# Slot attention: the next stage's weights sent in four pieces within the second pass, the context rows of group 2 sent before the first wait, and whole key transfers for all groups but the third

## The chip, the cores and the metric

The kernel runs on one core of one Trainium2 chip. The metric is the device time of one execution in microseconds. A core has TensorE (PE: matmuls into PSUM), the vector engine (DVE), ScalarE (ACT), GpSimd (POOL) and a sync engine (SP) that here only issues transfers. Transfers are issued on a queue of SP's or of ACT's own and are carried out by the same 16 DMA engines. The engines wait for each other by semaphores.

## What is computed

A network of four layers and twelve stages over 128 rows of 256 numbers, in which several stages attend to one context of 12544 keys. The change lies in the first stage, slot attention: three passes over all keys, each followed by a gated recurrent update of the 128 slots.

```
for _ in range(NUM_ITERS):                       # 3
    sn = rmsnorm(slots, slot_norm_w)
    q = jnp.einsum('bkd,ed->bke', sn, Wq)
    scores = jnp.einsum('bkd,bmd->bkm', q, k_proj) * scale
    attn = jax.nn.softmax(scores, axis=-2)
    attn = attn / (jnp.sum(attn, axis=-1, keepdims=True) + EPS)
    updates = jnp.einsum('bkm,bmd->bkd', attn, v_proj)
    slots = gru_cell(updates, slots, gru_wi, gru_wh, gru_bi, gru_bh)
```

`k_proj` and `v_proj` are projections of the context after a root-mean-square norm of each row. The softmax runs over the slots, so each key is a row of its own.

## The kernel before

**Tiles.** The 12544 keys are 14 groups of 896 (7 tiles of 128). A pass goes over the 14 groups; n counts them through the three passes, 0 to 41. Two layouts of the context are used. `ctxT` (numbers by keys, 896 KB a group) feeds the scores and is loaded anew in every pass into two buffers that alternate. `ctx_rows` (keys by numbers, 896 KB a group) feeds the weighted sum; it is loaded once, in pass 1, and kept.

**A group's way.** TensorE scores the group, first a half of 4 tiles and then one of 3 (`BANK_TILES`, L155 by way of `product`), and signals `scored` after each. The vector engine takes maxima (L531) and scales them by the roots `rinv` (L535). ScalarE takes the exponentials (L493), half by half, and signals `exp`. The vector engine normalises the probabilities (L545). TensorE multiplies them with the rows (`attend`, L388) and the vector engine adds the result to `pooled` (L549). TensorE's order is written out: score(n), then attend(n - 2), so at the start of a pass three groups are scored before the first attend.

**Only in pass 1** the roots are made: after the first half of exponentials of group n, ScalarE squares four tiles of the rows of group n + 1 (L486), the vector engine the other three (L558), and GpSimd raises the mean squares to -0.5 (L361, L363). The maxima of group n + 1 wait for its roots. The squares are written behind the home of the weights "patt", where "quant_up" comes later.

**SP's program** (L339 to L351) is one list of transfers in the order of n. For each n it waits until the half of group n - 2 that the buffer held has been scored, and sends the half (L346); then it sends the rows that `ROWS_AT` names for this n (L337). The 2560 KB of "gates" (weights of the update) follow at n = 10. Groups 0 and 1 need no wait. Each half has its own semaphore, `ctxT_in` with buffer and half, and TensorE waits for it before it scores the half.

**Weights of later stages** lie in one region with fixed homes (`HOMES`). `Weights.fetch` (L115) sends one whole and `Weights.wait` waits for its semaphore. "patt" (4100 KB, 8200 numbers on each of 128 partitions) is for the second stage and "quant_up" (768 KB) for the third; both are sent by ScalarE at the start of pass 2, before its first exponential. The vector engine rounds "quant_up" in small steps (`up.some`) in the spare time of passes 2 and 3.

**Before the first score** TensorE waits for the weights "slots", multiplies two of them (`fold_qk`, twice), transposes the slots and forms the query. `idle_products` (L171) multiplies the identity with constants into a bank that nobody reads.

## Time and profile before

| | us |
|---|---|
| median of three runs | 1555.98 |
| lowest and highest of them | 1551.15, 1556.0 |
| the profiled execution, time | 1554.31 |
| its span in the profile | 1552.4 |
| TensorE busy in it | 1441.7 (93%) |
| the vector engine, ScalarE, GpSimd busy | 929.9, 765.2, 80.9 |
| data moved | 182.30 MB, mean 117 GB/s |

The span is cut by time from its own start. Slot attention takes it from 4 to 326 us: first score at 13.53, second pass from 121.02, third from 230.05. A timeline row tells start, duration, engine, line, the operation with what it writes and reads, the number of instructions merged, and in brackets the engine's idle time just before and what ended it. The granted clock of TensorE is a share of 2.4 GHz, so 0.50 is 1.2 GHz. A line that a helper holds (L155, L346) has many users; the names of the tiles tell them apart. An fp32 matmul leaves two records.

### The profile page before, as it was taken

Reading aid. Unit: us, or ns where it says so; the run is one execution under the profiler, and the core shown is the slowest. Engines: PE = TensorE matmul, PEld = TensorE weight load, DVE = VectorE, ACT = ScalarE, POOL = GpSimd, SP = SyncE. Lnnn points to the kernel's source line nnn. Section 1 sums busy time; section 2 is a strip of 40 time slices with the busy share of each in tenths; the row PEclk is TensorE's granted clock in tenths of the full one; section 3 lists DMA queues with packets and bytes.
Section 4 is the critical chain, followed back from the end, with each engine's and each line's share of the span. In section 5 each row is a group of like instructions: output and inputs, shape, how many; then the busy total and the mean of one; then the engine's idle time right before and its main releaser. Section 6 shows DMA issues by size and latency. Waiting matters only on the chain. (4 is left out here: it accounts for less than half of the span.)

```text
span 1552.4 us, 29696 instructions
## 1 busy us (share of the span) xinstructions
PE 1441.7 (93%) x11376; PEld 1097.2 (71%) x11376; DVE 929.9 (60%) x2890; ACT 765.2 (49%) x1793; POOL 80.9 (5%) x78
## 2 busy tenths in 40 slices
PE   7997999988899789999999999999998798889987
PEld 6987989965677554677777677777776695656765
DVE  4754556656666432577777777777777375444434
ACT  5854536523122131467766676667667771323222
POOL 2310000000000000200000000000000000000000
PEclk9998999997999999999999999999999998989999
DMA  9946425311247289311111111110000301407860
GB/s 295 363 148 238 152 73 172 114 41 70 113 174 279 95 317 349 138 37 37 37 37 37 37 37 37 37 37 29 10 1 2 126 2 44 189 0 265 269 252 4
DMA packets 82812, 182.30 MB, mean 117 GB/s; under 512 B 5872, under 2 KB 58608, under 8 KB 81264
## 3 DMA queue, kind: packets, MB, share of 16 engines
q1 hardware_dynamic: 81952, 171.98, 31.5%
q10 hardware_dynamic: 720, 8.42, 1.3%
q8 instruction: 92, 1.51, 0.4%
q14 instruction: 48, 0.39, 0.1%
HBM read 179.86 MB, written 0.52 MB: 116 GB/s over the span
## 5 line engine op out<-in xcount | busy, mean ns | idle before, releaser
L2052 ACT ACTIVATE cross_s<-cross_s,cross_shift 128x896 f32<-128x896 f32 x224 | 215.1, 1031 | 35.1 <-DVE cross_shift L2136 35.1
L2046 ACT COPY cross_eT<-cross_ring 128x512 f32<-128x512 f32 x280 | 153.2, 591 | 143.2 <-PE cross_ring L1974 143.2
L1974 PEld LDWEIGHTS cross_ring<-consts,cross_s 128*128 128x128 f32 x1568 | 169.7, 142 | 58.8 <-issue 43.6
L1974 PE MATMUL cross_ring<-consts,cross_s 128*128 128x128 f32 x1568 | 198.3, 279 | 8.7 <-ACT cross_s L2052 8.7
L2127 DVE CUSTOM_DVE_ANT_0 cross_s<-cross_scores,cross_mask,cross_top 128x448 f32<-128x448 f32 x224 | 141.3, 680 | 83.2 <-PE cross_scores L1966 83.1
L493 ACT ACTIVATE slots_probs<-slots_scores,slots_bias,ctx_rinv 128x128 f32<-128x128 f32 x294 | 130.3, 458 | 105.1 <-DVE slots_bias L535 105.0
L155 PE MATMUL slots_scores<-slots_qkT,slots_ctxT 128*128 128x128 f32 x1176 | 142.0, 280 | 8.8 <-DMA slots_ctxT<-in_ctxT 8.2
L2127 DVE CUSTOM_DVE_ANT_0 cross_s<-cross_scores,cross_mask,cross_half_max 128x448 f32<-128x448 f32 x224 | 141.3, 680 | 14.7 <-PE cross_scores L1966 14.7
L155 PEld LDWEIGHTS slots_scores<-slots_qkT,slots_ctxT 128*128 128x128 f32 x1176 | 140.7, 197 | 12.3 <-DMA slots_ctxT<-in_ctxT 9.4
L388 PE MATMUL slots_attended<-ctx_rows,slots_probs 128*128 128x257 f32 x588 | 134.2, 380 | 2.4 <-DVE slots_probs L545 1.5
L388 PEld LDWEIGHTS slots_attended<-ctx_rows,slots_probs 128*128 128x128 f32 x588 | 108.6, 190 | 17.7 <-DVE slots_probs L545 1.9
L1966 PE MATMUL cross_scores<-cross_keysT,cross_qz 32*128 32x448 f32 x896 | 118.4, 586 | 1.3 <-DVE cross_qz L2097 1.3
L1988 PEld LDWEIGHTS cross_attended<-cross_eT,cross_values 128*32 128x32 f32 x3136 | 82.3, 110 | 38.0 <-issue 35.8
L531 DVE TENSOR_REDUCE slots_top<-slots_scores 128x4 f32<-128x512 f32 x84 | 52.4, 623 | 85.4 <-PE slots_scores L155 85.3
L1988 PE MATMUL cross_attended<-cross_eT,cross_values 128*32 128x128 f32 x3136 | 97.2, 274 | 2.3 <-ACT cross_eT L2046 1.7
L2109 DVE COPY cross_eT<-cross_ring 128x512 f32<-128x512 f32 x112 | 77.5, 692 | 34.4 <-PE cross_ring L1974 34.4
L155 PE MATMUL cross_ring<-weights_region,cross_ctxT 128*128 128x256 f32 x364 | 84.6, 384 | 0.0
L155 PE MATMUL cross_ring<-cross_ctxT,weights_region 128*128 128x448 f32 x208 | 83.5, 544 | 0.0
L155 PEld LDWEIGHTS cross_ring<-weights_region,cross_ctxT 128*128 128x128 f32 x364 | 67.0, 190 | 9.1
L1922 POOL TENSOR_SCALAR cross_mask<-cross_mask_int 128x896 f32<-128x896 int32 x14 | 44.9, 3205 | 458.0 <-DVE cross_top L2127 452.0
L1966 PEld LDWEIGHTS cross_scores<-cross_keysT,cross_qz 32*128 32x128 f32 x896 | 36.4, 182 | 38.3 <-issue 29.8
L493 ACT ACTIVATION_READ_ACCUMULATOR slots_probs<-slots_scores,slots_bias,ctx_rinv 128x1 f32 x294 | 60.0, 204 | 0.0
(805 smaller groups left out, 2111.2 us busy)
## 6 DMA issues: line engine op xcount, KB each, us to landing
ctx_rows<-in_ctx_rows SPq DMA_DIRECT2D x28, 896.0 KB, 7.7
ctx_rows<-in_moe_w SPq DMA_DIRECT2D x24, 1024.0 KB, 9.6
slots_ctxT<-in_ctxT SPq DMA_DIRECT2D x42, 512.0 KB, 4.0
slots_ctxT<-in_ctxT SPq DMA_DIRECT2D x42, 384.0 KB, 4.6
cross_ctxT<-in_ctxT SPq DMA_DIRECT2D x13, 896.0 KB, 4.7
padded_ctxT<-in_ctxT SPq DMA_DIRECT2D x12, 896.0 KB, 4.6
plain_ctxT<-in_ctxT SPq DMA_DIRECT2D x12, 896.0 KB, 4.7
local_layers<-in_w_local SPq DMA_DIRECT2D x2, 4552.0 KB, 13.8
```

Source lines behind the costliest of these rows:

```text
L155: last = pe.matmul(out, lhs, rhs, start=i == 0, stop=i == len(pairs) - 1)
L388: last = pe.matmul(at[b], probs[:, n % HELD, t], K.ctx[:, g * TILE + t, :], start=t == 0, stop=t == TILE - 1)
L493: last = act.activation(probs[:, a, t], sc[b][:, t], ACT.Exp, bias=bias[:, a, t:t + 1], scale=K.rinv[:, g * TILE + t:g * TILE + t + 1], ac ...
L531: dve.tensor_reduce(top[:, a, own], sc[b][:, own], X_AXIS, ALU.max).then_inc(st("top"), 1)
L1922: pool.tensor_scalar(mask[:, g % 2], mask_int[:, g % 2], 0.0, MASKED, ALU.is_equal, ALU.mult).then_inc(st("mask"), 1)
L1966: pe.matmul(scores(j), qz[rows, s // 2, s % 2], keysT[rows, g % 2, s // 2, half_keys(half)], start=True, stop=True).then_inc(st("scored"), 1)
L1974: last = pe.transpose(bank(("turn", u, t))[:, j * P:(j + 1) * P], s_buf[:, u % 2, j, t * P:(t + 1) * P], K.ident)
L1988: last = pe.matmul(attended[COLS * j:COLS * (j + 1), s * P:(s + 1) * P], values[:, g % 2, t, set_head(s, j)], eT[:, u % 2, t, j * P:(j + 1 ...
L2046: act.copy(eT[:, u % 2, t], bank(item)).then_inc(st("emptied_act"), 1)
L2052: act.activation(rows, rows, ACT.Exp, bias=shift[:, u % 2, j:j + 1], scale=SCALE).then_inc(st("exp"), 1)
L2109: dve.tensor_copy(eT[:, u % 2, t], bank(item)).then_inc(st("emptied_dve"), 1)
L2127: dve.tensor_tensor_reduce(s_buf[:, u % 2, j, half_keys(half)], scores(j), mask[:, g % 2, half_keys(half)], 1.0, so_far, ALU.add, ALU.max, ...
```

## The change

It has five edits, all in slot attention and the weights' fetch.

1. "patt" is sent as four pieces of 2050 columns (1025 KB each), by ScalarE after the exponentials of groups 3, 5, 7 and 9 of pass 2 (`PATT_AT`, `fetch_piece`); its semaphore counts four. "quant_up" is sent after the exponentials of group 0 of pass 2, with the same waits ahead of it.
2. `ROWS_AT`: the rows of group 2 go out at n = 1, right behind those of group 1. Rows 3 to 6 go out one a step at n = 2 to 5, rows 7 and 8 at n = 6, the others as before.
3. The keys of a group go out as one transfer when both halves of group n - 2 have been scored. Only the third group of each pass (`SPLIT_GROUP`) keeps its two halves and their two waits.
4. Two idle products stand ahead of TensorE's first wait.
5. The vector engine's steps on "quant_up" begin at group 4 of pass 2 instead of group 3, and one more is taken in pass 3.

```diff
--- before.py
+++ after.py
@@ -114,8 +114,13 @@
     def fetch(self, eng, name):
         eng.dma_start(self.buf(name), self.T[f"w_{name}"]).then_inc(self.arrived[name], 16)
 
+    def fetch_piece(self, eng, name, i, pieces):
+        spec, at = HOMES[name]
+        n = width(spec) // pieces
+        eng.dma_start(self.region[:, at + i * n:at + (i + 1) * n], self.T[f"w_{name}"][:, i * n:(i + 1) * n]).then_inc(self.arrived[name], 16)
+
     def wait(self, eng, name):
-        eng.wait_ge(self.arrived[name], 16)
+        eng.wait_ge(self.arrived[name], 16 * PIECES.get(name, 1))
 
 
 def linked(eng, sem):
@@ -240,8 +245,10 @@
 HELD = SLOT_LAG + 1
 ACT_ROWS = 4
 ROWS_SENT = 4
-ROWS_AT = {1: [1], 2: [2], 3: [3, 4], 4: [5, 6], **{n: [n + 2] for n in range(5, GROUPS - 2)}}
+ROWS_AT = {1: [1, 2], **{n: [n + 1] for n in range(2, 6)}, 6: [7, 8], **{n: [n + 2] for n in range(7, GROUPS - 2)}}
+PATT_AT = (3, 5, 7, 9)
 BANK_TILES = (range(0, 4), range(4, TILE))
+SPLIT_GROUP = 2
 
 
 class Quantise:
@@ -324,6 +331,12 @@
         def tiles(g):
             return slice(g * TILE, (g + 1) * TILE)
 
+        def sent_parts(n):
+            return BANK_TILES if n % GROUPS == SPLIT_GROUP else (range(TILE),)
+
+        def transfers(n, s):
+            return sum(len(sent_parts(m)) > s for m in range(n % 2, n + 1, 2))
+
         def rows_in(g):
             return st(f"rows_in{g % (ROWS_SENT + 1)}")
 
@@ -339,9 +352,9 @@
                 load_rows(0)
                 for n in range(SLOT_ITERS * GROUPS):
                     g, b = n % GROUPS, n % 2
-                    for s, part in enumerate(BANK_TILES):
+                    for s, part in enumerate(sent_parts(n)):
                         if n >= 2:
-                            sp.wait_ge(st("scored"), 2 * (n - 2) + s + 1)
+                            sp.wait_ge(st("scored"), 2 * (n - 2) + (s + 1 if g == SPLIT_GROUP else 2))
                         keys = slice(part[0] * P, part[-1] * P + P)
                         sp.dma_start(ctxT[:, b, :, keys], T["ctxT"][g:g + 1, :, :, keys].rearrange("o p c m -> p (o c) m")).then_inc(st(f"ctxT_in{b}{s}"), 16)
                     if n in ROWS_AT:
@@ -369,7 +382,8 @@
                 def score(n):
                     b = n % 2
                     for s, part in enumerate(BANK_TILES):
-                        pe.wait_ge(st(f"ctxT_in{b}{s}"), (n // 2) * 16 + 16)
+                        if s < len(sent_parts(n)):
+                            pe.wait_ge(st(f"ctxT_in{b}{s}"), 16 * transfers(n, s))
                         if n >= 2:
                             pe.wait_ge(st("exp"), 2 * (n - 2) + s + 1)
                         for t in part:
@@ -407,6 +421,7 @@
                 def update_slots(k):
                     pe.matmul(update, slotsT[:, k], wh[:, k, D:2 * D], start=False, stop=False)
 
+                idle_products(pe, K, scores[:, 1536:2048], 2)
                 K.weights.wait(pe, "slots")
                 fold_qk(0)
                 for it in range(SLOT_ITERS):
@@ -501,15 +516,16 @@
                     act.activation(small[:, 2:3], small[:, 1:2], ACT.Sqrt).then_inc(st("rms"), 1)
                     if it == 0:
                         squares(0)
-                    if it == 1:
-                        K.weights.fetch(act, "patt")
-                        act.wait_ge(st("squares_act"), ACT_ROWS * GROUPS)
-                        act.wait_ge(st("squares_dve"), (TILE - ACT_ROWS) * GROUPS)
-                        K.weights.fetch(act, "quant_up")
                     for g in range(GROUPS):
                         if g >= HELD:
                             act.wait_ge(st("attended"), it * GROUPS + g - HELD + 1)
                         exponentials(it * GROUPS + g)
+                        if it == 1 and g == 0:
+                            act.wait_ge(st("squares_act"), ACT_ROWS * GROUPS)
+                            act.wait_ge(st("squares_dve"), (TILE - ACT_ROWS) * GROUPS)
+                            K.weights.fetch(act, "quant_up")
+                        if it == 1 and g in PATT_AT:
+                            K.weights.fetch_piece(act, "patt", PATT_AT.index(g), PIECES["patt"])
                     act.wait_ge(st("reset_mm"), it + 1)
                     act.activation(gate[:, 0:D], reset, ACT.Sigmoid).then_inc(st("reset"), 1)
                     act.wait_ge(st("cand_in"), it + 1)
@@ -606,10 +622,10 @@
                             last.then_inc(st("gate_rows"), 1)
                         if g >= 1 + SLOT_LAG:
                             add(n - 1 - SLOT_LAG)
-                        if it == 1 and 3 <= g < GROUPS:
+                        if it == 1 and 4 <= g < GROUPS:
                             up.some(dve, 1)
                         if it == 2 and g < GROUPS:
-                            up.some(dve, 2 if g < 4 else 1)
+                            up.some(dve, 2 if g < 5 else 1)
 
                     link(dve.reciprocal(small[:, 5:6], pooled[:, D:D + 1]))
                     dve.tensor_scalar(diag[:, :], K.ident, small[:, 5:6], None, ALU.mult).then_inc(st("pooled"), 1)
@@ -3092,6 +3108,7 @@
     "delta": (DELTA_SPEC, max(DIAGONALS * P, width(FOLD_SPEC) + width(MOE_SPEC) + width(CROSS_SPEC))),
     "mqa": (MQA_SPEC, 0), "hashed": (HASH_SPEC, width(MQA_SPEC)),
 }
+PIECES = {"patt": 4}
 EARLY = {"padded": 2, "cross": 1, "plain": 2}
 EARLY_AT = {"padded": HOMES["padded"][1] + width(PADDED_SPEC), "cross": HOMES["cross"][1] + width(CROSS_SPEC) + SLOT_W1 + SLOT_W2,
             "plain": HOMES["hashed"][1]}
```

SP's queue at the start of the stage. Names: `ctx_rows` are the kept rows, `slots_ctxT` the key buffers; 128x2x512 is the first half of a group, 128x2x384 the second, 128x1792 a whole group. Before:

```order
L337 DMA ctx_rows<-in_ctx_rows 128x7x256
L346 DMA slots_ctxT<-in_ctxT 128x2x512
L346 DMA slots_ctxT<-in_ctxT 128x2x384
L346 DMA slots_ctxT<-in_ctxT 128x2x512
L346 DMA slots_ctxT<-in_ctxT 128x2x384
L337 DMA ctx_rows<-in_ctx_rows 128x7x256
L346 DMA slots_ctxT<-in_ctxT 128x2x512 [waits slots_scored]
L346 DMA slots_ctxT<-in_ctxT 128x2x384 [waits slots_scored]
L337 DMA ctx_rows<-in_ctx_rows 128x7x256
```

And now:

```order
L350 DMA ctx_rows<-in_ctx_rows 128x7x256
L359 DMA slots_ctxT<-in_ctxT 128x1792 x2
L350 DMA ctx_rows<-in_ctx_rows 128x7x256 x2
L359 DMA slots_ctxT<-in_ctxT 128x2x512 [waits slots_scored]
L359 DMA slots_ctxT<-in_ctxT 128x2x384 [waits slots_scored]
L350 DMA ctx_rows<-in_ctx_rows 128x7x256
L359 DMA slots_ctxT<-in_ctxT 128x1792 [waits slots_scored]
L350 DMA ctx_rows<-in_ctx_rows 128x7x256
```

The two key transfers of groups 0 and 1 are whole, rows of group 2 stand ahead of the first wait, and group 3's keys (the last but one row) wait for both halves of group 1.

ScalarE at the start of pass 2, from the root that the query needs (`slots_small`) on. The waits of a row stand in brackets. Before:

```order
L501 ACTIVATE slots_small<-slots_small 128x1 [waits slots_ms]
L115 DMA weights_region<-in_w_patt 128x8200
L115 DMA weights_region<-in_w_quant_up 128x1536 [waits slots_squares_dve,slots_squares_act]
L493 ACT_TABLE_LOAD
L493 ACTIVATE slots_probs,slots_total<-slots_scores,slots_bias,ctx_rinv 128x128 [waits slots_bias]
L493 ACTIVATE slots_probs,slots_total<-slots_scores,slots_bias,ctx_rinv 128x128 x3
L493 ACTIVATE slots_probs,slots_total<-slots_scores,slots_bias,ctx_rinv 128x128 [waits slots_bias]
L493 ACTIVATE slots_probs,slots_total<-slots_scores,slots_bias,ctx_rinv 128x128 x2
```

And now:

```order
L516 ACTIVATE slots_small<-slots_small 128x1 [waits slots_ms]
L508 ACT_TABLE_LOAD
L508 ACTIVATE slots_probs,slots_total<-slots_scores,slots_bias,ctx_rinv 128x128 [waits slots_bias]
L508 ACTIVATE slots_probs,slots_total<-slots_scores,slots_bias,ctx_rinv 128x128 x3
L508 ACTIVATE slots_probs,slots_total<-slots_scores,slots_bias,ctx_rinv 128x128 [waits slots_bias]
L508 ACTIVATE slots_probs,slots_total<-slots_scores,slots_bias,ctx_rinv 128x128 x2
L115 DMA weights_region<-in_w_quant_up 128x1536 [waits slots_squares_dve,slots_squares_act]
```

Both weight transfers stood ahead of the table load and the first exponential; now "quant_up" follows the seven exponentials of the first group. The first piece of "patt" stands behind those of the fourth, in front of the fifth's:

```order
L508 ACTIVATE slots_probs,slots_total<-slots_scores,slots_bias,ctx_rinv 128x128 [waits slots_bias]
L508 ACTIVATE slots_probs,slots_total<-slots_scores,slots_bias,ctx_rinv 128x128 x2
L120 DMA weights_region<-in_w_patt 128x2050
L508 ACTIVATE slots_probs,slots_total<-slots_scores,slots_bias,ctx_rinv 128x128 [waits slots_bias,slots_attended]
L508 ACTIVATE slots_probs,slots_total<-slots_scores,slots_bias,ctx_rinv 128x128 x3
```

The other three pieces stand in the same way behind groups 5, 7 and 9.

## Rows read from the trace of the kernel before

**Rows 1.** Stretches: length, busy us (records) of PE, PEld, DVE, ACT, POOL, clock, DMA share, GB/s.

```profile
13.53:106.73 93.20, 89.90 (x588) 82.63 (x589) 61.07 (x199) 66.69 (x301) 26.67 (x42) 0.98 0.87 295
121.02:217.48 96.46, 89.08 (x589) 83.43 (x589) 49.33 (x122) 45.97 (x197) 0.00 (x0) 0.95 0.53 176
230.05:316.42 86.37, 86.37 (x590) 80.89 (x590) 52.43 (x128) 45.89 (x197) 0.00 (x0) 1.00 0.42 129
```

**Rows 2.** Timeline of TensorE at the starts of passes 2 and 3.

```profile
134.81 5.85 PE L155 MATMUL slots_scores<-slots_qkT,slots_ctxT 128*128 128x128 f32 x28 [7.38 <-DMA slots_ctxT<-in_ctxT]
140.50 3.21 PE L388 MATMUL slots_attended<-ctx_rows,slots_probs 128*128 128x257 f32 x14
...
239.43 3.21 PE L388 MATMUL slots_attended<-ctx_rows,slots_probs 128*128 128x257 f32 x14
```

**Rows 3.** Stretches of 1 us, TensorE alone: busy (records), clock, DMA share, GB/s.

```profile
130.00:131.00 1.00, 0.00 (x0) 0.50 0.96 395
...
140.00:141.00 1.00, 1.00 (x9) 1.00 0.75 172
```

**Rows 4.** Transfers, 117 to 134.8: queue, packets, MB, share; issues, KB, us to landing.

```profile
q10 hardware_dynamic: 288, 4.98, 69.9%
q1 hardware_dynamic: 789, 1.40, 20.8%
...
weights_region<-in_w_patt ACTq DMA_DIRECT2D x1, 4100.0 KB, 14.0
...
slots_ctxT<-in_ctxT SPq DMA_DIRECT2D x2, 384.0 KB, 11.0
```

**Rows 5.** Transfers issued at 233 to 235, at 19 to 20, and in a later stage.

```profile
slots_ctxT<-in_ctxT SPq DMA_DIRECT2D x1, 384.0 KB, 4.6
...
ctx_rows<-in_ctx_rows SPq DMA_DIRECT2D x1, 896.0 KB, 7.8
...
padded_ctxT<-in_ctxT SPq DMA_DIRECT2D x12, 896.0 KB, 4.6
```

**Rows 6.** Timeline of TensorE, start of the stage and pass 1.

```profile
5.93 2.08 PE L155 MATMUL slots_mm<-weights_region 128*128 128x256 f32 x4 [5.93 <-DMA weights_region<-in_w_slots]
...
10.72 1.13 PE L155 MATMUL slots_attended<-slots_qk_weight,slots_slotsT 128*128 128x256 f32 x4 [0.58 <-DVE slots_qk_weight L563]
...
25.93 3.31 PE L388 MATMUL slots_attended<-ctx_rows,slots_probs 128*128 128x257 f32 x14 [0.83 <-DVE slots_probs L545]
...
33.00 3.31 PE L388 MATMUL slots_attended<-ctx_rows,slots_probs 128*128 128x257 f32 x14 [0.64 <-DVE slots_probs L545]
...
40.12 3.28 PE L388 MATMUL slots_attended<-ctx_rows,slots_probs 128*128 128x257 f32 x14 [0.69 <-DVE slots_pooled L549]
...
46.97 3.21 PE L388 MATMUL slots_attended<-ctx_rows,slots_probs 128*128 128x257 f32 x14
...
81.52 3.39 PE L155 MATMUL slots_scores<-slots_qkT,slots_ctxT 128*128 128x128 f32 x28 [0.50 <-DMA slots_ctxT<-in_ctxT]
```

**Rows 7.** Stretches, TensorE alone, columns as in rows 3.

```profile
128.00:134.80 6.80, 0.00 (x0) 0.63 1.01 399
42.00:66.00 24.00, 23.66 (x164) 1.00 1.06 357
16.00:18.00 2.00, 2.00 (x15) 0.72 0.10 30
```

**Rows 8.** Timeline of SP's queue, the issues of two transfers.

```profile
19.16 0.61 SPq L337 DMA_DIRECT2D ctx_rows<-in_ctx_rows  x1
...
66.90 1.19 SPq L115 DMA_DIRECT2D weights_region<-in_w_gates  x1
```

**Rows 9.** Timeline of ScalarE and GpSimd in pass 1.

```profile
26.99 0.42 ACT L486 ACTIVATE weights_region<-ctx_rows 128x256 f32<-128x256 f32 x1 [1.31 <-DMA ctx_rows<-in_ctx_rows]
...
29.07 1.48 POOL L363 TENSOR_TENSOR ctx_rinv<-slots_ms,slots_power 128x7 f32<-128x7 f32 x1
...
34.72 1.48 POOL L363 TENSOR_TENSOR ctx_rinv<-slots_ms,slots_power 128x7 f32<-128x7 f32 x1
```

## Prediction

> **What bounds the kernel now.** The edits touch the first stage, slot attention, which runs three passes over 14 groups of keys. I read the table of stretches first [rows 1]: the part of passes 1, 2 and 3 from the first score to the last attend. All three do the same TensorE work (588 to 590 matmul records), and only pass 3 is TensorE without a gap: 86.37 us busy of 86.37, clock 1.00, 6.17 us a group. So pass 3 is the floor and the others show their losses: pass 2 takes 96.46, which is 10.09 too long, and pass 1 takes 93.20, which is 6.83 too long. TensorE bounds the stage; where it stands still, the time adds to the end. The later stages keep their instructions and start when this one ends.
>
> Pass 2's loss is in one place. In TensorE's timeline [rows 2] it waits 7.38 us for keys at the third group, and then needs 5.7 us for that group's 28 records (134.81 to 140.50), where pass 3 needs 9.38 for three groups, 3.1 each. The clock's rows [rows 3] say why: granted 0.50 (1.2 GHz) after TensorE had stood still, 1.00 (2.4 GHz) again only at 140. From 121.02 to the first attend at 140.50 are 19.48 us; in pass 3 they are 9.38, from 230.05 to 239.43 [rows 1, 2]. The difference, 10.10, is the whole loss of pass 2. The cause is in the transfers [rows 4]: the smaller half of a group's keys took 11.0 us to land where it takes 4.6 in pass 3 [rows 5], because the next stage's weights, 4100 KB that landed after 14.0 and another 768 KB, were sent on ScalarE's queue just before the first score.
>
> Pass 1's loss is spread [rows 6]. Attends start at 25.93, 33.00, 40.12 and 46.97, so 12.40 us from the first score (9.38 in pass 3), then 7.07, 7.12 and 6.85 where 6.17 is the floor: losses of 3.02, 0.90, 0.95 and 0.68. A wait of 0.50 at 81.52, behind the gates' weights, is the next. These are 6.05 of the 6.83; the rest lies around the gates and at the end of the pass.
>
> **Part 1, weights in pieces.** The big transfer leaves the start of pass 2 and goes out as four of 1025 KB, after the exponentials of groups 3, 5, 7 and 9; the 768 KB one goes after those of group 0. Without them the third group's halves land as in pass 3, and TensorE reaches the first attend 10.1 us earlier: the half clock goes with the wait. What is late next is the fourth group's keys: one transfer, issued when the second group is scored and needed 6.17 later. A whole 896 KB transfer lands in 4.6 in a later stage [rows 5]; the 768 KB now beside it add 0.786 MB at 399 GB/s, the rate of the crowded stretch [rows 7], so 2.0 us. 4.6 + 2.0 is 6.6 against 6.17: a wait between 0 and 0.5, I take 0.3.
> The pieces: a steady group's keys are issued when the group two before is scored (3.1 us of its 6.17) and needed 12.34 - 3.1 = 9.2 us later. 4.6 plus the whole of a piece, 1.05 MB at 399 GB/s = 2.6, is 7.2. That leaves 2.0 us, so the pieces cost nothing; the cover is TensorE's own two attends and one score, and if it were gone a piece would cost its 2.6. Their issue lies on a ScalarE that is busy 46 of 96 us [rows 1]. Nothing reads these weights before the next stage. The vector engine's rounding steps move by one group in a pass where it is busy 49 of 96: nothing.
> Part 1: -10.1 + 0.3 = **-9.8 us**.
> The queues' rows [rows 4] also show what a turn carries: 288 packets took 4.98 MB on ScalarE's queue (17 KB each), 789 took 1.40 MB on sync's (1.8 KB each). The Trainium skill, "DMA: Bandwidth & Descriptors", section "Queues, rings and completion order", says that a DMA engine takes turns between the queues packet by packet. By that rule the keys starved for their small packets, and whole transfers beside quarter pieces, with packets of like size, would share evenly: the sum stays, and rival (c) loses weight.
>
> **Part 2, rows sent ahead.** Rows of group 2 now go out with those of group 1, before sync first waits for a score. Today they are issued at 19.2 [rows 8] and land 7.8 later, at 27.0 [rows 5], and ScalarE, which squares them, waits for them: its squares start at 26.99 after 1.31 idle [rows 9]. The DMA engines stood nearly empty from 16 to 18 us, 30 GB/s for the 357 of full stretches [rows 7]; the rows (0.92 MB at 357, 2.6 us) fill that hole and land near 19.5. Then GpSimd's root for group 2, which ends at 30.55 [rows 9], ends 1.3 earlier, and attend 1 is released by TensorE itself: 33.00 becomes 32.1. The root of group 3 follows one loop later (36.20 - 30.55 = 5.65), so at 34.9 for 36.2, and attend 2 with it: 40.12 becomes 38.8. For attend 3 the keys come in time, since the rows of groups 6 and 7 no longer stand ahead of them: 6.17, so 44.9 for 46.97, **-2.1 us**. The third group's own halves now queue behind the moved rows: 18.7 + 1.5 + about 1 is 21.2, when TensorE gets to them at 21.7. No cost.
>
> **Part 3, one transfer per group but the third.** The first half of a group's keys goes out 1.3 us later than now, the second at the same time. In steady parts the 9.2 us cover it, in all three passes. It bites where the slack is short, behind the gates' weights. There TensorE wanted the first half at 81.0 and got it at 81.5 [rows 6]; the second (0.39 MB at 357) came 1.1 later. A whole transfer ends with the second: a wait of 1.6 for 0.5, unless the queue is less full than now. It is: the filled hole moves its work 2 us or more forward while TensorE moves 2.1. From its own issue, 1.2 us before the gates' at 66.90 [rows 8], the chain is 65.7 + 4.6 (keys) + 2.6 (rows) + 6.6 (gates, 2.62 MB at 399) + 2.3 (keys) = 81.8. Between -0.1 and +1.1; I take **+0.2**.
>
> **Part 4, two idle products.** They run from 4.1 to 6.1 by the duration of four such records at 5.93, 2.08 us [rows 6], where TensorE waits for weights until 5.93 anyway: **+0.1**. Whether they bring the full clock earlier is the first rival.
>
> Sum: -9.8 - 2.1 + 0.2 + 0.1 = -11.6 us. The profiled execution took 1554.3 (span 1552.4 and 1.9 around it), so it becomes **1542.7**. It stood 1.7 under the median of the three runs and 3.2 over their lowest; I keep 1542.7.
>
> **Rivals.** (a) The idle products warm the clock. For it: four records of 256 columns take 2.08 us from 5.93 and 1.13 from 10.72 [rows 6], after TensorE has been busy for a while; starting 1.8 us earlier could bring the rise before the second fold, which lies on the path, and start the scores at 12.1 for 13.53. Against it: the clock falls again, to a mean of 0.72 in 16 to 18 [rows 7], and the third group's keys do not land before 21, so the first attend comes at 24.1 at best, for 25.93. TensorE then runs ahead of the transfers and waits longer at the gates, 1.1. Net -1.8 - 0.3 (no wait at attend 2) + 1.1 = -1.0: 1541.7, or 1540.6 without that longer wait.
> The Trainium skill, "TensorE: Matmul & The Clock Gate", section "What's actually happening", says that the throttled clock is the default and activity releases it; by that rule this rival happens.
> (b) The transfers collide more than I say, without a fall of the clock: 0.5 at the fourth group for 0.3, 1.1 at the gates for 0.2, 1 us in pass 1 because the rows of groups 5 to 7 go out later than now, and half of part 2 missing (1.0). Together +3.1: 1545.8.
> (c) Slower: each piece holds up the keys beside it as the whole did. If they landed after 11.0 as in [rows 4], TensorE would wait 11.0 - 9.2 = 1.8 and lose 2.6 more at half clock (5.7 - 3.1), 4.4 four times, 17.6: 1560.3. It beats the gain from 2.9 us a piece on. Against it: a piece is a fifth of what did that.
> (d) The moved rows and idle products do nothing at all: 1544.8.
>
> **Numbers.** The forecast 0.42, (a) 0.27, (b) with (d) 0.28, (c) 0.03. The range runs from 1538.5 ((a) at its best, less the 1.7 between runs) to 1548 ((b), plus as much). A measurement tells 0.3%, 4.7 us, from no change; all but (c) lie beyond it: faster 0.95, same 0.03, slower 0.02.
>
> **What would show it.** Part 1: pass 2's stretch at 86.4 to 87.2 with clock 1.00, no wait for keys above 0.5, four pieces landing in 5 to 8 us. Part 2: rows of group 2 landing near 19.5, no ScalarE idle before their squares, attends 6.17 apart but for the second. Part 3: one wait of 0.4 to 1.6 behind the gates. Part 4: first score at 13.5 (12.1 by rival a). Pass 1's stretch at 91 to 92. It is wrong if pass 2 stays over 90, or if a stage behind this one changes its length by more than 1 us.

## The result, and the profile after

The changed kernel took **1546.19 us** (median of 20 runs, 1540.65 to 1551.29) beside 1555.57 for the kernel before (20 runs, 1548.13 to 1559.38): a ratio of 0.9944, 95% interval 0.9932 to 0.9956, so 9.4 us faster. The profiled execution took 1549.58 us with a span of 1547.7, which is 3.4 over its own median. The span before was 1552.4, so the two profiled executions differ by 4.7 us only; where these lie is told behind the experiments.

The three passes, from the first score to the last attend, in the table of stretches that [rows 1] has for the kernel before (columns as there):

```profile
15.76:106.87 91.11, 89.61 (x588) 82.76 (x589) 60.92 (x199) 66.58 (x301) 26.71 (x42) 1.00 0.83 294
121.16:211.01 89.85, 86.89 (x589) 81.03 (x589) 49.11 (x121) 45.98 (x197) 0.00 (x0) 1.00 0.56 200
223.58:310.45 86.87, 86.62 (x589) 80.96 (x589) 52.61 (x129) 45.88 (x197) 0.00 (x0) 1.00 0.38 128
```

Pass 1 went from 93.20 to 91.11, pass 2 from 96.46 to 89.85, pass 3 from 86.37 to 86.87. Pass 2 is still 3 us or more above its floor of 86.4 to 86.9, and TensorE's timeline shows the loss in two waits on the third group's keys, where [rows 2] had one of 7.38:

```profile
121.16 6.41 PE L160 MATMUL slots_scores<-slots_qkT,slots_ctxT 128*128 128x128 f32 x56
128.58 2.05 PE L160 MATMUL slots_scores<-slots_qkT,slots_ctxT 128*128 128x128 f32 x16 [1.01 <-DMA slots_ctxT<-in_ctxT]
132.58 1.60 PE L160 MATMUL slots_scores<-slots_qkT,slots_ctxT 128*128 128x128 f32 x12 [1.95 <-DMA slots_ctxT<-in_ctxT]
134.03 3.21 PE L402 MATMUL slots_attended<-ctx_rows,slots_probs 128*128 128x257 f32 x14
137.07 3.29 PE L160 MATMUL slots_scores<-slots_qkT,slots_ctxT 128*128 128x128 f32 x28
```

The first 14 records of the attend after the waits take 3.21 us, and the granted clock reads 1.00 in every stretch of 1 us from 128 to 135, so the clock did not fall here. The fourth group's keys, for which I had forecast the wait, made none (137.07 has no bracket). They landed 7.1 us after their issue, later than the 6.6 I had for them, but TensorE itself came 3 us late by then. The transfers issued from 117 to 134.8, to be held against [rows 4], and then those issued while a piece was sent, 141 to 147 (queue: packets, MB, share; issue: KB, us to landing):

```profile
q1 hardware_dynamic: 688, 1.84, 31.4%
q10 hardware_dynamic: 144, 0.79, 12.3%
...
slots_ctxT<-in_ctxT SPq DMA_DIRECT2D x2, 896.0 KB, 5.8
weights_region<-in_w_quant_up ACTq DMA_DIRECT2D x1, 768.0 KB, 6.8
slots_ctxT<-in_ctxT SPq DMA_DIRECT2D x1, 512.0 KB, 5.4
slots_ctxT<-in_ctxT SPq DMA_DIRECT2D x1, 384.0 KB, 8.1
...
q1 hardware_dynamic: 144, 0.92, 44.8%
q10 hardware_dynamic: 135, 1.03, 42.9%
...
weights_region<-in_w_patt ACTq DMA_DIRECT2D x1, 1025.0 KB, 6.8
slots_ctxT<-in_ctxT SPq DMA_DIRECT2D x1, 896.0 KB, 5.2
```

The second half of the third group (384 KB) landed 8.1 us after its issue, for 11.0 before and 4.6 undisturbed [rows 4, 5]. ScalarE's timeline tells what met it:

```profile
124.06 0.46 ACT L508 ACTIVATE slots_probs<-slots_scores,slots_bias,ctx_rinv 128x128 f32<-128x128 f32 x1 [4.68 <-DVE slots_bias L551]
...
125.29 0.20 ACT L508 ACTIVATION_READ_ACCUMULATOR slots_probs<-slots_scores,slots_bias,ctx_rinv 128x1 f32 x1
125.34 0.38 ACTq L115 DMA_DIRECT2D weights_region<-in_w_quant_up  x1
...
127.03 0.22 ACT L508 ACTIVATION_READ_ACCUMULATOR slots_probs<-slots_scores,slots_bias,ctx_rinv 128x1 f32 x1
```

The code puts this transfer after the seven exponentials of group 0. They end at 127.25, but the issue stands at 125.34, while the third of the seven ends: ScalarE's queue hands the transfer out while activations ahead of it in the program still have to run. The other two profiles of this kernel show the same, and so does the first piece, issued at 141.21 during the exponentials of group 3. The issue at 125.34 is about 1 us behind that of the half that landed late (between 124.4 and 124.6), and 1.9 earlier than the code reads.

Pass 1's steps add up to what was forecast: attends at 28.29, 34.95, 41.11 and 47.29, so steps of 6.66, 6.16 and 6.18, 19.0 in sum, where [rows 6] gave 7.07, 7.12 and 6.85, 21.0 in sum. The wait behind the gates is 0.31 for 0.50:

```profile
28.29 3.31 PE L402 MATMUL slots_attended<-ctx_rows,slots_probs 128*128 128x257 f32 x14 [0.36 <-DVE slots_probs L561]
...
34.95 3.21 PE L402 MATMUL slots_attended<-ctx_rows,slots_probs 128*128 128x257 f32 x14
...
41.11 3.22 PE L402 MATMUL slots_attended<-ctx_rows,slots_probs 128*128 128x257 f32 x14
...
47.29 3.21 PE L402 MATMUL slots_attended<-ctx_rows,slots_probs 128*128 128x257 f32 x14
...
81.66 3.39 PE L160 MATMUL slots_scores<-slots_qkT,slots_ctxT 128*128 128x128 f32 x28 [0.31 <-DMA slots_ctxT<-in_ctxT]
```

The mechanism that was forecast for these steps is there too. ScalarE has no idle time before it squares the rows of group 2, and GpSimd's root for them, which follows, ends at 31.49:

```profile
30.01 1.48 POOL L376 TENSOR_TENSOR ctx_rinv<-slots_ms,slots_power 128x7 f32<-128x7 f32 x1
```

That is 15.73 us after the first score, for 17.02 before (30.55 less 13.53): 1.3 earlier, as forecast.

The pass begins 2.2 us later than before, though (15.76 for 13.53). In this execution the weights "slots" landed about 1.1 us later (first product of the fold at 6.98 for 5.93), and the query's products, with the transposes behind them, ran at half rate (another 1.2):

```profile
6.98 2.08 PE L160 MATMUL slots_mm<-weights_region 128*128 128x256 f32 x4 [0.70 <-DMA weights_region<-in_w_slots]
...
9.27 1.91 PE L160 MATMUL slots_mm<-weights_region 128*128 128x256 f32 x4
11.76 2.08 PE L160 MATMUL slots_attended<-slots_qk_weight,slots_slotsT 128*128 128x256 f32 x4 [0.58 <-DVE slots_qk_weight L579]
```

In [rows 6] the row that answers to the last took 1.13. The slow query products stand in no other profiled execution of any kernel here; weights that came late do in two more (6.83 and 6.56). Neither is laid to the change, and together they are 2.2 of the 3.4 by which this execution stands over the median. The granted clock reads 1.00 over these rows, so the half rate is told from their durations alone.

### The profile page after: what moved, and what is told of

Read it like the earlier page. It is cut to its first block and busy times, and to the rows that moved or that the text cites. A ratio compares the mean times of both kernels' runs of the same rounds, so it can differ in the third digit from the quotient of the medians.

```text
span 1547.7 us, 29631 instructions
## 1 busy us (share of the span) xinstructions
PE 1442.9 (93%) x11380; PEld 1096.2 (71%) x11380; DVE 929.7 (60%) x2890; ACT 765.1 (49%) x1793; POOL 80.9 (5%) x78
```

## The experiments

All were timed beside the kernel before on the same chip (before: 1554.69, 1555.24 and 1555.40 in the three sets), and each left one profiled execution. The changed kernel itself was in the first and the third set; runs of the second set are held against all 32 runs of it. Theory Q is the one from the trace above: what is left of pass 2's loss is the 768 KB transfer, issued into the third group's halves.

**The changed kernel again**, in the first and the third set.

> The changed kernel once more, as the base of this call and as a second sample of its start. Theory L (luck at the start): the late first score of the first execution (15.8 us for 13.5 in the kernel before) is no part of the change; here it may come anywhere between 12.5 and 16, and the time is 9 us under the kernel before. Theory P (the products): the two idle products hold the fold back, so the first score is again past 15 us. Both: TensorE again waits near 1.0 and 1.9 us for the third group's halves in pass 2, whose stretch takes 89 to 90 us.

> The changed kernel beside the two that follow, on one chip. Both theories: 1545.5 to 1546.5 as the earlier runs of it, pass 2 between 88.5 and 90 us with key waits of 1.8 to 3.0 us on the third group and none after.

Measured: 1545.54 (1540.68 to 1551.84; 0.9940, 0.9921 to 0.9959) and 1546.37 (1543.15 to 1548.86; 0.9940, 0.9923 to 0.9957). Waits in pass 2: 0.99 + 0.86 and 0.76 + 1.78, both times on the third group; the pass took 88.74 and 89.43. First scores at 13.28 and 13.56: the late start of the first profile was luck.

**The 768 KB two groups later**, twice.

```diff
-                        if it == 1 and g == 0:
+                        if it == 1 and g == 2:
                             act.wait_ge(st("squares_act"), ACT_ROWS * GROUPS)
```

> The changed kernel with the 768 KB weights sent after the exponentials of group 2 of pass 2 instead of group 0. Theory Q (those 768 KB hold the third group's two halves up, since ScalarE's queue issues them 1.8 us before the last exponential of the group ends): both waits go, pass 2's stretch falls from 89.9 to 86.4 to 86.9, and the time falls by 3.0 us against the changed kernel (ratio about 0.992 to the kernel before). Rival W (the whole transfers of groups 3 and on, which stand in sync's queue, hold the halves up): the waits stay at 2 us or more and the time does not move.

> The kernel of e1_up_late once more (in_w_quant_up sent two groups later), beside the changed kernel on this chip. Theory Q (the wait is the 768 KB meeting the third group's halves): 2 to 4 us below the changed kernel, key waits in pass 2 below 1.0 us in sum, pass 2 at 86.4 to 87.5 us. Rival (the 3 us of the first pair was luck of the run): within 1 us of the changed kernel's time.

Measured: 1542.88 (1537.18 to 1547.39; 0.9922, 0.9904 to 0.9941) and 1544.28 (1539.57 to 1548.23; 0.9926, 0.9908 to 0.9943), 2.7 and 2.1 under the changed kernel on the same chip. The means of the 12 runs of each differ by 2.6 +- 2.7 us; against all 32 runs of the changed kernel the 12 are 2.8 +- 2.3 lower. The profile shows where: the wait before the second half is gone in both, and pass 2 takes 87.44 and 87.67. TensorE's timeline of the second run, then the transfers it issued from 118 to 136:

```profile
118.85 6.41 PE L160 MATMUL slots_scores<-slots_qkT,slots_ctxT 128*128 128x128 f32 x56
126.31 3.39 PE L160 MATMUL slots_scores<-slots_qkT,slots_ctxT 128*128 128x128 f32 x28 [1.04 <-DMA slots_ctxT<-in_ctxT]
129.54 3.21 PE L402 MATMUL slots_attended<-ctx_rows,slots_probs 128*128 128x257 f32 x14
```

```profile
weights_region<-in_w_quant_up ACTq DMA_DIRECT2D x1, 768.0 KB, 5.5
slots_ctxT<-in_ctxT SPq DMA_DIRECT2D x1, 512.0 KB, 5.4
slots_ctxT<-in_ctxT SPq DMA_DIRECT2D x1, 384.0 KB, 5.1
```

The second half lands after 5.1 for 8.1. Theory Q holds for the second wait. The first half still lands after 5.2 to 5.4 with no weights under way (issue of the 768 KB at 130.60), and costs 0.8 to 1.0.

**The same transfer, only held back until the exponentials have ended.**

```diff
                         if it == 1 and g == 0:
+                            act.wait_ge(st("exp"), 2 * GROUPS + 2)
                             act.wait_ge(st("squares_act"), ACT_ROWS * GROUPS)
```

> The changed kernel with one more wait ahead of the 768 KB transfer: ScalarE first waits until its own last exponential of group 0 has ended. The prediction had put the issue there (127.1 on the time scale of the kernel before), while the trace shows it 1.8 us earlier, in the middle of the seven exponentials. Theory Q: issued 1.8 us later, it no longer meets the third group's second half: that one lands 4.6 to 5.5 after its issue for 6.9 and 8.1, and the wait falls on the fourth group's keys, 0 to 0.5 us as predicted; pass 2's stretch 87 to 88, 1 to 2 us under the changed kernel. Rival T (the 1.8 us are too little, what counts is the turn-taking of two queues with any transfer of the third or fourth group): total waits in pass 2's first four groups stay at 1.8 us or more, only later in place.

Measured: 1547.81 (1541.41 to 1550.23; 0.9941, 0.9921 to 0.9961). This is the place at which I had supposed the issue. TensorE's timeline, then the issue in ScalarE's:

```profile
127.53 3.39 PE L160 MATMUL slots_scores<-slots_qkT,slots_ctxT 128*128 128x128 f32 x28 [0.92 <-DMA slots_ctxT<-in_ctxT]
130.75 3.21 PE L402 MATMUL slots_attended<-ctx_rows,slots_probs 128*128 128x257 f32 x14
134.38 3.39 PE L160 MATMUL slots_scores<-slots_qkT,slots_ctxT 128*128 128x128 f32 x28 [0.42 <-DMA slots_ctxT<-in_ctxT]
```

```profile
126.07 0.22 ACT L508 ACTIVATION_READ_ACCUMULATOR slots_probs<-slots_scores,slots_bias,ctx_rinv 128x1 f32 x1
126.31 0.38 ACTq L115 DMA_DIRECT2D weights_region<-in_w_quant_up  x1
126.75 0.46 ACT L508 ACTIVATE slots_probs<-slots_scores,slots_bias,ctx_rinv 128x128 f32<-128x128 f32 x1 [0.46 <-ACT slots_probs L508]
```

With the issue behind the exponentials the wait on the second half is gone and one of 0.42 stands at the fourth group, where the prediction had 0.3. So the mechanism and the size were right for the place I thought of, and the place was wrong. In the time nothing can be told from the changed kernel (the means agree within 0.2, +- 3); pass 2 took 88.24 here, and 88.74 to 89.85 in the changed kernel.

**The pieces alone** on the kernel before: the edits of part 1 (four pieces, the 768 KB after group 0's exponentials, the rounding steps), with the old rows, halves everywhere and no idle products.

```diff
-                    if it == 1:
-                        K.weights.fetch(act, "patt")
...
                         exponentials(it * GROUPS + g)
+                        if it == 1 and g == 0:
...
+                            K.weights.fetch(act, "quant_up")
+                        if it == 1 and g in PATT_AT:
+                            K.weights.fetch_piece(act, "patt", PATT_AT.index(g), PIECES["patt"])
```

> The kernel before with the weights' edit alone: four pieces of the 4100 KB and the 768 KB after group 0, all key transfers in halves, rows in the old order, no idle products. By my steps it carries nearly the whole gain: pass 2's stretch 89 to 91 for 96.5, -6 to -7.5 us, ratio 0.9955. Rival W: with halves everywhere the pieces' large packets starve the keys' small ones, so TensorE waits up to 2 us behind each of the four pieces and pass 2 stays at 92 to 98.

Measured: 1548.69 (1547.13 to 1549.24; 0.9958, 0.9945 to 0.9971), 6.0 us under before. Pass 2 takes 90.73. TensorE's timeline, then the stretches of 1 us (busy, clock, DMA share, GB/s):

```profile
130.81 1.73 PE L160 MATMUL slots_scores<-slots_qkT,slots_ctxT 128*128 128x128 f32 x12 [2.42 <-DMA slots_ctxT<-in_ctxT]
132.33 4.81 PE L394 MATMUL slots_attended<-ctx_rows,slots_probs 128*128 128x257 f32 x14
```

```profile
131.00:132.00 1.00, 1.00 (x10) 1.00 1.01 380
132.00:133.00 1.00, 1.00 (x6) 0.58 1.01 384
133.00:134.00 1.00, 1.00 (x3) 0.50 0.34 112
```

86.4 (the floor) + 2.42 (the wait) + 1.6 (14 products in 4.81 for 3.21) is 90.4 of the 90.73. The half clock came after this one wait; after the changed kernel's 1.01 and 1.95, with 16 records between, it did not. At the pieces themselves TensorE never waits, though the 384 KB halves of that stretch need 7.0 us in the median. No run sends the 4100 KB whole at a later place, so how much of the gain is the place and how much the cutting is not shown.

**The rows alone, and the rows put back.** First the new table on the kernel before, then the old table on the changed kernel.

```diff
-ROWS_AT = {1: [1], 2: [2], 3: [3, 4], 4: [5, 6], **{n: [n + 2] for n in range(5, GROUPS - 2)}}
+ROWS_AT = {1: [1, 2], **{n: [n + 1] for n in range(2, 6)}, 6: [7, 8], **{n: [n + 2] for n in range(7, GROUPS - 2)}}
```

> The kernel before with the new order of the rows alone. By my steps attends 0 to 3 of pass 1 are 6.2, 6.6 and 6.2 apart (7.07, 7.12, 6.85 before), pass 1's stretch is 91 for 93.2, and the time is 2.1 us lower, ratio 0.9987, at the edge of what five rounds tell. Rival: the moved rows hold up the third group's halves in sync's queue, TensorE waits for them and the first attend comes as much later as the next ones gain: stretch 93, ratio 1.000.

> The changed kernel with the old table of context rows (one row group late in the places 1 to 6). Theory R (the rows sent ahead are worth what the first pass lost before): the late rows come back, pass 1 is 92 to 93.5 us instead of 90.4 to 91.1, and the time is 1.5 to 2.5 us above the changed kernel's. Rival (what the rows give, the clock or the next wait takes back, as where they were put alone): pass 1 is longer but the time within 1 us of the changed kernel's.

Measured: alone 1554.0 (12 runs, 1549.51 to 1559.63; 0.9995, 0.9984 to 1.0006); put back 1549.95 (1547.06 to 1551.77; 0.9962, 0.9947 to 0.9977), 3.6 over the changed kernel on the same chip (against all 32 runs of it the means differ by 3.3 +- 2.0). With the old table the attends of pass 1 drift apart again. TensorE's timeline of the kernel with the rows put back:

```profile
31.57 3.21 PE L402 MATMUL slots_attended<-ctx_rows,slots_probs 128*128 128x257 f32 x14
35.81 3.39 PE L160 MATMUL slots_scores<-slots_qkT,slots_ctxT 128*128 128x128 f32 x28 [1.03 <-DMA slots_ctxT<-in_ctxT]
39.04 3.21 PE L402 MATMUL slots_attended<-ctx_rows,slots_probs 128*128 128x257 f32 x14
43.25 3.39 PE L160 MATMUL slots_scores<-slots_qkT,slots_ctxT 128*128 128x128 f32 x28 [1.01 <-DMA slots_ctxT<-in_ctxT]
46.48 3.21 PE L402 MATMUL slots_attended<-ctx_rows,slots_probs 128*128 128x257 f32 x14
```

Steps of 7.47 and 7.44 for 6.16 and 6.18; the pieces alone, with the same table, have 7.62 and 7.46. So the rows are worth 2.6 us in those two steps, and it is the keys, queued behind rows that were not yet needed, that end them.

Alone on the kernel before, the moved rows did what was expected in the trace: steps of 6.27, 6.50 and 6.24, 19.0 in sum for 21.0. Pass 1 was even shorter than that (13.52 to 102.90, so 89.38 for 93.20), but 1.3 of these 3.8 us lie ahead of the first attend, where the first scores happened to run at full clock. That part varies by itself: from the first score to the first attend the thirteen profiled executions took 11.1 to 13.6 us. From the first attend to the end of the pass they took 80.80 before, 81.55 and 81.11 in the two other kernels with the old table, and 78.1 to 79.3 with the new table, with one exception (below, without idle products). So the rows are worth about 2.5 us in the trace, with the other edits or without. The median alone moved by 0.7 only, the means by 0.8 +- 1.8, which 2.1 does not contradict, nor is it far enough from 3.3 +- 2.0 to be called another value. In that one profile pass 3 also began with products at half rate (L405, the reset gate's product, took 1.90 for 1.03, the first 84 records of scores 10.38 for 9.5) and was 0.8 longer; one profile can't tell whether this is the rule.

The moved rows have a price, too, that the prediction put at nothing. With the old table TensorE never waited for the third group's keys in pass 1. With the new one it waited 0.41 and 0.80 in two of the changed kernel's three profiles, 0.85 with the rows alone, and 1.58 to 2.21 in four of the other variants, whose first scores had run at full clock.

**Halves everywhere** in the changed kernel (part 3 undone).

```diff
-            return BANK_TILES if n % GROUPS == SPLIT_GROUP else (range(TILE),)
+            return BANK_TILES
-                            sp.wait_ge(st("scored"), 2 * (n - 2) + (s + 1 if g == SPLIT_GROUP else 2))
+                            sp.wait_ge(st("scored"), 2 * (n - 2) + s + 1)
```

> The changed kernel with every group's keys in two halves again (84 transfers), all else kept. My step for this part said +0.2 us for whole transfers, so -0.2 here, nothing that can be told: ratio 0.994. In the trace: behind the gates' weights the wait is 0 to 0.5, while the pieces' packets of 8 KB meet keys' packets of 2 KB, so that the halves beside a piece land in 6 to 8 us for the 4.6 of a whole transfer, still inside their 9.2. Rival W2 (whole transfers carry a gain of their own, by fewer and larger packets in the full stretches of pass 1): pass 1's stretch is 1 us or more longer than the 90.4 to 91.1 of the changed kernel.

Measured: 1547.45 (1544.52 to 1550.13; 0.9947, 0.9932 to 0.9962). The means differ from the changed kernel's by 1.1 +- 1.9: nothing that can be told. But the transfers differ. In the window from 110 to 165 of this kernel, and then of the changed one:

```profile
slots_ctxT<-in_ctxT SPq DMA_DIRECT2D x8, 512.0 KB, 4.8
slots_ctxT<-in_ctxT SPq DMA_DIRECT2D x7, 384.0 KB, 7.5
weights_region<-in_w_patt ACTq DMA_DIRECT2D x2, 1025.0 KB, 7.1
```

```profile
slots_ctxT<-in_ctxT SPq DMA_DIRECT2D x6, 896.0 KB, 4.6
weights_region<-in_w_patt ACTq DMA_DIRECT2D x2, 1025.0 KB, 6.5
```

Taken one by one over the whole pass, the four halves of 384 KB that go out within about 1 us ahead of a piece landed after 7.9, 8.2, 7.4 and 7.9, the ones between them after 4.5 to 5.6. The four whole transfers of 896 KB at the same places landed after 4.6, 4.6, 4.5 and 4.6. A whole transfer goes out when the second half would, so the group is complete some 3 us earlier beside a piece. Neither makes TensorE wait, since 9.2 us are there. The wait behind the gates was 0.50 with halves and 0.31, 0.82 and 0.34 in the three profiles with whole transfers.

**Without the idle products, and with three more** (the latter on the kernel with the late 768 KB).

```diff
-                idle_products(pe, K, scores[:, 1536:2048], 2)
```

> The changed kernel without the two idle products at the stage's start. Theory L: the products do nothing for the clock, since in two executions of the changed kernel the first score came at 15.8 and at 13.3, with or without them the same band; time within 1 us of the changed kernel, ratio 0.994. Rival a of the prediction (they bring the full clock earlier): without them the first fold and the second run at half rate and the first score never comes before 13.5; time 1 us higher.

```diff
                         fold_qk(1)
+                        idle_products(pe, K, scores[:, 1536:2048], 1)
...
+                    if it == 0:
+                        idle_products(pe, K, scores[:, 1536:2048], 1)
...
+                    else:
+                        idle_products(pe, K, scores[:, 1536:2048], 1)
```

> The version with the 768 KB after group 2 (0.992 before), and three more idle products, one in each gap of TensorE between the second fold and the first score, where it stands still 0.6 us three times. Theory F (the half clock over the first scores comes from these gaps): no records at half rate after the fold, first scores at full rate; since the third group's keys do not land before about 21 and the roots chain holds the rest, the first attend comes at 24.1 to 24.5 and the time is 0 to 1.5 us under the version without. Rival: at half clock each product lasts 0.9 us and pushes the query back by 0.3 to 0.5 each, the first score comes at 14 or later and the time is 1 us higher.

Measured: without them 1546.8 (1540.4 to 1550.98; 0.9941, 0.9921 to 0.9961), with three more 1542.94 (1540.87 to 1546.89; 0.9923, 0.9906 to 0.9941), the mean 0.1 from that of the 12 runs of the late 768 KB alone. Over all profiled executions the first score stands at 13.21 to 13.53 without idle products (four) and at 12.65 to 15.76 with two (eight). With three more it is 12.56, the earliest of all, with no product at half rate behind the first fold, as theory F said, and the first attend at 23.89. But the time is the same.

For the clock, the second fold tells most. It took 1.03 (full rate) in two of the eight, with first scores at 12.65 and 13.11, and in the one with three more; in none of the four without. That is too few to tell it from luck, and it gained nothing at the first attend of the two: TensorE reached the third group before its keys, waited 1.95 and 2.21, fell to half clock, and attended at 25.98 and 26.69, where the kernel before had 25.93.

Two more things stand in these profiles. Without idle products TensorE waited 2.09 for the fourth group's keys in pass 1, which took 92.90: the new table does not always keep the keys in time. With three more, pass 2 had no wait for keys at all (86.36), its first half having landed after 4.1.

Pass by pass, from one profiled execution of each (us; waits are TensorE's for keys of the third or fourth group of pass 2; the median is that of the set in which the profile was taken):

| kernel | first score | pass 1 | waits, pass 2 | pass 2 | pass 3 | median |
|---|---|---|---|---|---|---|
| before | 13.53 | 93.20 | 7.38 | 96.46 | 86.37 | 1555.57 |
| rows alone | 13.52 | 89.38 | 7.18 | 96.68 | 87.19 | 1554.0 |
| pieces alone | 13.21 | 92.68 | 2.42 | 90.73 | 86.59 | 1548.69 |
| changed, rows put back | 13.78 | 92.23 | 1.17 + 0.81 | 88.87 | 86.37 | 1549.95 |
| changed, halves | 13.11 | 91.86 | 0.50 + 2.69 | 91.74 | 86.37 | 1547.45 |
| changed | 15.76 | 91.11 | 1.01 + 1.95 | 89.85 | 86.87 | 1546.19 |
| changed, 768 KB late | 13.49 | 91.31 | 0.80 | 87.44 | 86.86 | 1542.88 |

The 4.7 us between the profiled executions of before and changed are: first score +2.2, pass 1 -2.1, pass 2 -6.6, pass 3 +0.5, everything behind the three passes +1.3. The last is no work of the change: it took 1235.98 before, 1237.25, 1235.68 and 1238.07 in the changed kernel, and 1231.99 to 1238.15 over all thirteen.

By the times, the parts add up: 6.0 for the pieces alone and 3.3 to 3.6 for the rows on top of the rest, beside 9.4 for all. Whole key transfers and idle products are worth nothing that can be told.

## Why the prediction was right, and where it was not

I had 1542.7 and a range of 1538.5 to 1548; it came to 1546.19, inside the range and 3.5 over the point, and nearer to rivals (b) and (d) than to the sum. (By its own terms the range would be 1538.9 to 1547.5; it was rounded outward.) The direction and the places were right. Against its own median the change brought 9.4 where the sum had 11.6; the other 1.3 is the base, since I started from an execution that stood 1.3 under the median of the 20 runs.

**Part 1** (-9.8) is the mis-sized term. The trace of before was read rightly: the wait of 7.38 and the half clock behind it came from the two transfers, and pass 2 fell by 6.6 (96.46 to 89.85) in the profile, and the median by 6.0 with the pieces alone. The step that failed is "the third group's halves land as in pass 3 ... what is late next is the fourth group's keys", with +0.3 for it. I took "after the exponentials" for the moment at which these end. The issue comes 1.9 us before that and meets the third group's second half: waits of 1.95, 0.86 and 1.78 in the three profiles of the changed kernel. With the issue held back, the wait was 0.42 at the fourth group, as I had said, and with it two groups later it was gone. The remaining wait of 0.8 to 1.2 is the first half's late landing, for which I had no term and have no cause.

The pieces cost nothing, as forecast: landed after 6.2 to 6.8, no wait beside them, rival (c) fell. I had allowed the keys 7.2 us beside a piece, and they took 4.5 to 5.2: what matters is not the bytes alone. Keys of 144 packets and 0.92 MB (6.4 KB a packet) stood beside 135 packets and 1.03 MB (7.6 KB). The late half of the third group had small packets (the mean of its queue, with a whole transfer in it, is 2.7 KB) beside 5.5 KB. The halves everywhere show it once more, 7.4 to 8.2 beside a piece against 4.5 or 4.6. The Trainium skill, "DMA: Bandwidth & Descriptors", section "Queues, rings and completion order", says that a DMA engine takes turns between the queues packet by packet. By that rule a transfer of small packets loses against one of large packets, and these landings agree; no run changed the size of the packets alone, or shows whether the packets that the profile counts are the ones by which turns are taken. I had used that rule for the pieces only and not for the one transfer that stood beside halves.

**Part 2** (-2.1): right in kind and size. The root of group 2 came 1.3 earlier, as forecast. The step into attend 1 gave 0.4 (forecast 0.9), and the next two gave 7.12 + 6.85 - 6.16 - 6.18 = 1.6, so 2.0 in sum, and the stretch 2.1. Against the two kernels with the old table and the pieces those two steps alone give 2.6 and 2.7, and the time 3.3 to 3.6: rather small there. Wrong was the "No cost" at the third group's keys: in two of three profiles TensorE waited for them, 0.41 and 0.80, and more in the variants. Pass 1's stretch, 91.11, 90.39 and 90.98, is at the lower edge of the 91 to 92 that I gave or just under it.

**Part 3** (+0.2): 0.31, 0.82 and 0.34 behind the gates for 0.50 before, so +0.0 on average, within the -0.1 to +1.1. **Part 4** (+0.1): nothing that can be told. Rival (a), the warmer clock, fell for this kernel, with the first score at 13.3 to 15.8 in its three profiles where the rival needed 12.1. In the two variants whose second fold ran at full rate, what I had set against it held: the third group's keys landed at 21.1 and 21.8, and nothing was left of the gain at the first attend. Rival (d) (1544.8) was right about the idle products and wrong about the rows. Rival (b) gave nearly the right time (1545.8) by a mechanism of the right kind, collisions without a fall of the clock, but put 0.5 of it at the fourth group and the rest in pass 1, whose stretch came out as long as forecast or shorter; the collision that cost the time was at the third group of pass 2.

One sentence in "what would show it" was too sharp: a later stage that changes by more than 1 us as a sign of error. From the cross stage's first keys to the end the instructions are the same in all kernels, and the stretch took 929.90 in the kernel before, 933.00 and 932.40 in the changed one, 929.10 and 931.90 with the late 768 KB. It moves by 4 us without any edit, and all that lies behind the three passes by 6 us, so a stage's length in one profile is no sign of error at that size. Runs of one kernel lie as far apart: 1540.65 to 1551.29 in the 20 of the changed one, a standard deviation of 2.9.

The best version of these is the changed kernel with the 768 KB two groups later, 0.9922 and 0.9926 of before, with or without more idle products.

## What to carry to other kernels

Read from the queue's rows when a transfer is issued, and not from the place of its line: behind a row of activations it can go out while they still run, so where its moment matters it needs a wait on what the code puts before it, or a place a whole step later. Price a transfer beside a critical one by packets as well as bytes; here the critical one did best with large packets or with nothing beside it. When one cause of a stall is taken out, look at what is issued within the microsecond around the transfer that was late; what is next in line was found there rather than at the next group. And when one profile is held against another, compare a part that does not move by itself: here the stretch behind the first attend told the worth of the rows in every profile but one, while the part ahead of it moved by 2.5 us from execution to execution.

## What the runs showed of the hardware

- ScalarE's queue issued a transfer at 125.34 while four of the seven exponentials ahead of it in the program, the last ending at 127.25, had yet to run. With a wait on the last of them ahead of it, it went out at 126.31, just behind their end.
- 384 KB of keys landed after 4.6 in pass 3 of before and after 4.5 to 5.1 in pass 2 with the 768 KB two groups later, after 7.4 to 8.2 beside pieces of 1025 KB, 6.9 to 8.3 beside the 768 KB and 11.0 beside 4100 KB, while a whole group of 896 KB took 4.5 or 4.6 beside the same pieces.
- A stall of TensorE of about 2 us may or may not be followed by half clock (1.2 GHz). In pass 2 stalls of 2.42 and 2.69 us were (14 records in 4.81 and 4.14 us for 3.21), and ones of 1.95 and 2.10 were not. In pass 1 a stall of 2.09 was not, but ones of 1.95, 2.14 and 2.21 were (28 records in 5.02 us for 3.39). So the length of the stall alone does not decide.
- The third group's first half of pass 2 (512 KB) landed after 4.0 or 4.1 in three of the profiled executions and after 5.2 to 5.6 in the seven others with whole transfers, and that also where no weights were sent near it (5.2 and 5.4 with the 768 KB two groups later, but 4.1 in the one with more idle products). TensorE waited for each of the late ones 0.8 to 1.2 us. The cause is open.
